# A token mixer beside routed experts: router logits in fp32, another order of VectorE's work, and a last step in halves

## The chip, the core and the metric

The kernel runs on one core of a Trainium2 chip. The metric is the device time of one execution in microseconds (us). The core has TensorE (PE, matrix products), VectorE (DVE), ScalarE (ACT), GpSimd (POOL) and SyncE (SP); each works through its own queue in order, and semaphores tie the queues together.

## The reference, cut to what matters

The input is x of shape (16, 256, 128): 4096 tokens of 128 channels. It is layer-normed to xn. Two branches read xn, and out = x + s * silu(f).

```python
# branch f: four rounds of routed experts, on cur (4096 x 128), starting at xn
for r in range(4):
    logits = cur @ Wg[r] + bg[r]                     # 4 experts
    vals, idx = top_k(logits, 2); w = softmax(vals)  # cw: w at idx, 0 elsewhere
    hmid = gelu(einsum('nh,ehf->enf', cur, W1) + b1) # all 4 experts, 512 wide
    y = einsum('enf,efh->enh', hmid, W2) + b2
    cur = cur + einsum('ne,enh->nh', cw, y)
# branch s, for each of the 16 sequences: r, w, k, v, alpha, g are linear maps of
# xn mixed with its predecessor; state = state * decay + alpha*k*v along time;
# mixed = r * state, normed in groups of 8 channels, times g, then @ W_out.T + b_out
```

Everything is fp32.

## The kernel before

The tokens form 8 blocks of 512 (two sequences each). `cur` holds the state of the experts' branch, channels on partitions, tokens along the row. A **turn** is one round on one block: 32 turns, k = 0 to 31, the eight blocks in order four times. A turn has four **steps**, one for each expert: 128 steps, s = 4k + e. Products are in fp32r, a form of fp32 with fewer bits that TensorE takes at full pace; to keep precision each operand is split into a high and a low part (`cur_hi`, `cur_lo`, `g_hi`, `g_lo`, `w1_hi`, `w1_lo` and so on), and three products of parts are added: hi*hi, lo weights*hi, hi weights*lo.

One step s:
- TensorE `up(s)`: 12 matmuls of 128x512 into the four banks `hb`.
- ScalarE `hidden(s)`: four gelu (L382), two copies to `g_hi` of 1024 columns (L386), in two halves; between the halves it does other small work: `router_tanh`, `end_tanh`.
- VectorE `g_low_half(s, 0)` and `(s, 1)` (L619): `g_lo` = g - `g_hi`.
- TensorE `down(s)` (L909, L910, L914): 12 matmuls into `yb[s % 2]`, the eight with `g_hi` first, then the four with `g_lo`. It waits for `combine(s - 2)`, which frees the bank.
- VectorE `combine(s)` (L633): (y + b2) times the expert's gate, broadcast over partitions in `cw_b`, into `tmp`; a DMA from GpSimd's queue adds `tmp` into `cur` (L322). The last two steps are added by VectorE (L642).

TensorE's queue in step s is `up(s+1)`, then for the late steps `turn_product`, then `down(s)`, then `logits(n)` at the steps of `LOGITS_AT`, then one stage of the mixer. VectorE's queue in step s is the norm statistics of the first steps, `split_cur`, mixer work, `g_low_half(s+1, 0)`, `g_low_half(s+1, 1)`, `router_scores`, `router_gates`, `combine(s)`. The queues are written out by hand; the tables `LOGITS_AT`, `SPLIT_AT`, `NORM_SCALE` say at which step something stands.

**The router.** Turns are taken in batches (`BATCHES`): two of two turns, seven of four. `logits(n)` does, for each turn of a batch, two matmuls of 128x512 with `wg_pad`: the gate weights' high and low parts, 8 columns, stand in 128 columns of zeros, and a shifted window puts turn i's rows at partition 32i of `rb`, all turns adding up in one bank. `router_scores(n)` (L579 to L598) transposes `rb` in blocks of 32x32, adds the two parts and the bias, ranks the experts; `router_tanh` and `router_gates` make the gates; DMAs on SP's queue (`spread_gates`) write them to a scratch and broadcast them into `cw_b`. The logits batches stand at steps 0, 6, 12, 28, 44, 60, 76, 92 and 108; scores are made one step later, gates two steps later. combine(0) and combine(8), the first steps whose gates come from the first two batches, are done at the end of the following step (`LATE`).

**The mixer.** Each sequence m goes through 8 stages, one a step, from step 15 + 7m: three projections into `pb`, the scan (stage 3), the group norm `mixer_norm` (stage 4, some 20 small VectorE instructions), the gate and the output projection (stage 6). Stage 0 of a sequence shares a step with stage 7 of the one before.

**The end of a block.** In the last round, block b is final after step 103 + 4b. `end_tanh(b)` on ScalarE, `end_scaled(b)` and `end_product(b)` on VectorE make z = s * silu(f), `turn_product(b)` on TensorE transposes it into `rb`, `end_output(b)` adds x, and SP's queue stores it. For b = 0 to 6 these stand at steps 101 + 4b (tanh), 102 + 4b (scaled, product) and 103 + 4b (turn, output), among the steps of the next block but one that is still computed. Block 7's follow behind step 127.

## Time and profile before

| | us |
|---|---|
| median of 3 runs | 824.88 |
| lowest and highest | 821.72, 825.96 |
| the profiled execution | 823.14 |
| its span, first to last instruction | 821.3 |
| TensorE busy | 803.9 |
| VectorE busy | 714.8 |
| ScalarE busy | 652.2 |

A profile is one execution. Busy time is the time in which at least one instruction of the engine runs; a matmul's end is modelled, and matmuls overlap, so the pace of TensorE is read from the starts. The mean granted clock of TensorE is 0.993 of full.

### The profile page before, as it was taken

How to read it: one execution, taken by the hardware profiler on the slowest of the kernel's cores; microseconds unless marked ns; L12 is line 12 of the kernel's file. 1: busy time of each engine (PE TensorE's matmuls, PEld its weight loads, DVE VectorE, ACT ScalarE, POOL GpSimd, SP SyncE). 2: the span in 40 equal slices, each digit the busy share in tenths (PEclk: the TensorE clock that was granted, in tenths of full speed). 3: DMA queues.
4: the chain of work that ended last, by engine and by line, in shares of the span. 5: the costliest groups of instructions: out<-in, count | busy, mean ns of one | idle time of the engine just before them, and what ended most of it. 6: DMA issues, size and time to landing. Idle time of an engine off the chain costs nothing. (4 is left out here: it accounts for less than half of the span.)

```text
span 821.3 us, 10635 instructions
## 1 busy us (share of the span) xinstructions
PE 803.9 (98%) x3656; PEld 651.3 (79%) x3656; DVE 714.8 (87%) x1339; ACT 652.2 (79%) x911; POOL 115.0 (14%) x135
## 2 busy tenths in 40 slices
PE   8899999999999999999999999999999999899996
PEld 7787788888788887888888887888878888678885
DVE  6978888889997979988898898898989898889897
ACT  7798887887887877888788886888778887678874
POOL 0010211111111111111111101111111111011110
PEclk9999999999999999999999999999999999999998
DMA  9333463342533415423164422644226343174532
GB/s 255 116 78 91 102 162 84 96 97 39 143 59 83 97 33 142 103 49 94 29 152 100 95 39 39 142 103 104 39 54 164 93 116 72 19 180 115 129 65 51
DMA packets 44468, 78.50 MB, mean 96 GB/s; under 512 B 6656, under 2 KB 23552, under 8 KB 40448
## 3 DMA queue, kind: packets, MB, share of 16 engines
q0 software_dynamic: 18144, 33.04, 23.9%
q1 hardware_dynamic: 25136, 44.64, 16.5%
q8 instruction: 29, 0.48, 0.2%
q10 hardware_dynamic: 1136, 0.16, 0.1%
q14 instruction: 23, 0.19, 0.1%
HBM read 40.34 MB, written 2.36 MB: 52 GB/s over the span
## 5 line engine op out<-in xcount | busy, mean ns | idle before, releaser
L382 ACT ACTIVATE g<-h_bank,b_c 128x512 f32<-128x512 f32 x512 | 329.3, 681 | 80.2 <-PE h_bank L853 78.5
L619 DVE TENSOR_TENSOR g_lo<-g,g_hi 128x1024 fp32r<-128x1024 f32 x256 | 307.9, 1221 | 73.6 <-ACT g_hi L386 72.6
L386 ACT ACTIVATE g_hi<-g 128x1024 fp32r<-128x1024 f32 x256 | 271.7, 1062 | 8.1
L322 POOL DMA_DIRECT2D cur<-tmp x126 | 113.9, 904 | 692.1 <-DVE tmp L633 572.4
L849 PE MATMUL h_bank<-cur_hi,w_hi 128*128 128x512 f32 x512 | 206.3, 403 | 1.2 <-ACT g L382 0.7
L909 PE MATMUL y_bank<-g_hi,w_hi 128*128 128x512 f32 x512 | 203.4, 397 | 2.8 <-issue 2.2
L853 PE MATMUL h_bank<-cur_lo,w_hi 128*128 128x512 f32 x512 | 204.1, 399 | 0.0
L850 PE MATMUL h_bank<-cur_hi,w_lo 128*128 128x512 f32 x512 | 203.1, 397 | 0.0
L910 PE MATMUL y_bank<-g_hi,w_lo 128*128 128x512 f32 x512 | 203.0, 397 | 0.0
L914 PE MATMUL y_bank<-g_lo,w_hi 128*128 128x512 f32 x512 | 140.9, 396 | 2.2 <-DVE g_lo L619 2.2
L909 PEld LDWEIGHTS y_bank<-g_hi,w_hi 128*128 128x128 f32 x512 | 96.5, 188 | 26.5 <-issue 2.6
L914 PEld LDWEIGHTS y_bank<-g_lo,w_hi 128*128 128x128 f32 x512 | 96.3, 188 | 26.2 <-DVE g_lo L619 3.1
L853 PEld LDWEIGHTS h_bank<-cur_lo,w_hi 128*128 128x128 f32 x512 | 96.6, 189 | 23.7 <-DVE cur_lo L567 0.4
L910 PEld LDWEIGHTS y_bank<-g_hi,w_lo 128*128 128x128 f32 x512 | 96.6, 189 | 23.4
L849 PEld LDWEIGHTS h_bank<-cur_hi,w_hi 128*128 128x128 f32 x512 | 97.0, 189 | 20.5 <-ACT g L382 1.1
L850 PEld LDWEIGHTS h_bank<-cur_hi,w_lo 128*128 128x128 f32 x512 | 96.7, 189 | 19.2
L633 DVE SCALAR_TENSOR_TENSOR tmp<-y_bank,b_c,cw_b 128x512 f32<-128x512 f32 x128 | 94.9, 743 | 1.4 <-DMA cur<-tmp 1.3
L653 DVE SCALAR_TENSOR_TENSOR xm<-xx,mix,xn_t 128x256 f32<-128x256 f32 x96 | 42.0, 479 | 0.6
L661 DVE TENSOR_TENSOR xm_lo<-xm,xm_hi 128x512 fp32r<-128x512 f32 x48 | 33.2, 693 | 1.6
L853 PE MATMUL p_bank<-xm_lo,pj_hi 128*128 128x256 f32 x96 | 27.6, 288 | 0.9 <-DVE xm_lo L661 0.9
L849 PE MATMUL p_bank<-xm_hi,pj_hi 128*128 128x256 f32 x96 | 27.5, 286 | 0.8 <-DVE xm_hi L659 0.8
L850 PE MATMUL p_bank<-xm_hi,pj_lo 128*128 128x256 f32 x96 | 27.0, 281 | 0.0
(120 smaller groups left out, 516.9 us busy)
## 6 DMA issues: line engine op xcount, KB each, us to landing
cur<-tmp POOLq DMA_DIRECT2D x126, 256.0 KB, 3.4
cw_b<-cw_scratch SPq DMA_DIRECT2D x31, 1024.0 KB, 5.1
cur<-in_x SPq DMA_DIRECT2D x8, 256.0 KB, 5.5
xn_t<-cur SPq DMA_DIRECT2D x8, 256.0 KB, 2.8
xr<-in_x SPq DMA_DIRECT2D x8, 256.0 KB, 3.2
out<-o SPq DMA_DIRECT2D x7, 256.0 KB, 2.4
cw_b<-in_w SPq DMA_DIRECT2D x4, 256.0 KB, 5.2
cw_b<-cw_scratch SPq DMA_DIRECT2D x1, 768.0 KB, 5.2
```

Source lines behind the costliest of these rows:

```text
L322: pool.dma_start(cur[:, block_of(s // E)], tmp[:, s % 2, :], accum_op=ALU.add).then_inc(summed, DMA)
L382: nc.scalar.activation(g[:, gb, ft * BLK:(ft + 1) * BLK], hb[ft][:, :], ACT.Gelu_apprx_tanh, bias=b1_c[:, e * FT + ft:e * FT + ft + 1]).th ...
L386: nc.scalar.activation(g_hi[:, gb, h], g[:, gb, h], ACT.Copy).then_inc(g_hi_done, 1)
L619: nc.vector.tensor_tensor(g_lo[:, gb, h], g[:, gb, h], as_f32(g_hi[:, gb, h]), ALU.subtract).then_inc(g_lo_done, 1)
L633: nc.vector.scalar_tensor_tensor(out=tmp[:, s % 2, :], in0=yb[s % 2][:, :], scalar=b2_c[:, e:e + 1], in1=cw_b[:, q, e * BLK:(e + 1) * BLK] ...
L653: last = nc.vector.scalar_tensor_tensor(out=xm[:, n, :], in0=xx[:, :], scalar=mix[:, k:k + 1], in1=xs[:, 1:LEN + 1], op0=ALU.mult, op1=ALU ...
L849: nc.tensor.matmul(out_ap, w_hi, v_hi, start=True, stop=False)
L850: nc.tensor.matmul(out_ap, w_lo, v_hi, start=False, stop=False)
L853: return nc.tensor.matmul(out_ap, w_hi, v_lo, start=False, stop=True)
L909: nc.tensor.matmul(yb[b][:, :], w2_hi[:, e * FT + ft, :], hi, start=(ft == 0), stop=False)
L910: nc.tensor.matmul(yb[b][:, :], w2_lo[:, e * FT + ft, :], hi, start=False, stop=False)
L914: last = nc.tensor.matmul(yb[b][:, :], w2_hi[:, e * FT + ft, :], g_lo[:, b, ft * BLK:(ft + 1) * BLK], start=False, stop=(ft == FT - 1))
```

## The change

- `logits(n)`: instead of two fp32r matmuls with 128 columns of weights a turn, one fp32 matmul with 32 columns (`wg_p`: the 4 gate weights and zeros) reads `cur` itself and writes to the partitions 32i to 32i + 31 of `rb`. The split of the gate weights, the copies into `wg_pad` and one add in `router_scores` are gone.
- VectorE's order: combine(0) stands ahead of the norm statistics of step 1, combine(8) between the two `g_low_half` of step 9. low_w2(2) and router_gates(0) stand at the start of step 0. router_scores (for n >= 3) and `end_scaled` stand between the two halves, `end_product` behind them, and both end pieces one step earlier, at 101 + 4b; `turn_product` and `end_output` move to step 102 + 4b. In step 110, the one step with a mixer norm two steps after a logits batch, `mixer_norm` goes behind the `g_low_half`.
- The last step: `down_last` makes the 512 tokens in two halves of 256, the first in `yb[1]`, the second in `hb[3]`, and combine, add, tanh, scale, product, transposes follow by halves; the output was by halves already.

```diff
+def behind_router(s):
+    return s - 2 in LOGITS_AT.values()
...
+        last_y = (yb[(STEPS - 1) % 2], hb[FT - 1])
...
-            if s > END_FROM and (s - END_FROM) % E == 3:
+            if s > END_FROM and (s - END_FROM) % E == 2:
                 r_jobs["end", (s - END_FROM) // E] = len(r_jobs)
...
+            act.wait_ge(r_full, r_jobs["end", NB - 3] + 1)
+            for n in range(2):
+                h = slice(n * HALF, (n + 1) * HALF)
+                act.wait_ge(half_added, n + 1)
+                nc.scalar.activation(th[:, (NB - 1) % 2, h], cur[:, TOK - BLK + n * HALF:TOK - BLK + (n + 1) * HALF], ACT.Tanh,
+                                     scale=0.5).then_inc(half_th, 1)
...
-                if k == 0 or k % NB == QUADS - 1 and k > NB:
-                    nc.vector.tensor_scalar(wg_pad[:, WG_AT:WG_AT + 2 * E], as_f32(wg_hl[:, k // NB, :]), 1.0, None,
-                                            ALU.mult)
...
-                link(nc.vector.tensor_tensor(l3, lgt[p, :, 0:E], lgt[p, :, E:2 * E], ALU.add))
-                link(nc.vector.tensor_tensor(l3, l3, bg3, ALU.add))
+                link(nc.vector.tensor_tensor(l3, lgt[p, :, 0:E], bg3, ALU.add))
...
-                if s >= STEPS - ADDED_BY_DVE:
+                if s == STEPS - 2:
                     last = cur[:, block_of(k)]
                     dve.wait_ge(summed, DMA * (STEPS - ADDED_BY_DVE))
                     dve.wait_ge(combined, s + 3)
-                    if s > STEPS - ADDED_BY_DVE:
-                        dve.wait_ge(added, s - STEPS + ADDED_BY_DVE)
...
+            def combine_half(n):
+                k, e = TURNS - 1, E - 1
+                q = k % 2
+                dve.wait_ge(half_down, n + 1)
+                dve.wait_ge(cwb_ready[q], DMA * (k // 2 + 1))
+                dve.wait_ge(summed, DMA * (STEPS - ADDED_BY_DVE))
+                part = tmp[:, (STEPS - 1) % 2, n * HALF:(n + 1) * HALF]
+                nc.vector.scalar_tensor_tensor(out=part, in0=last_y[n][:, 0:HALF], scalar=b2_c[:, e:e + 1],
+                                               in1=cw_b[:, q, e * BLK + n * HALF:e * BLK + (n + 1) * HALF],
+                                               op0=ALU.add, op1=ALU.mult).then_inc(half_combined, 1)
+                last = cur[:, TOK - BLK + n * HALF:TOK - BLK + (n + 1) * HALF]
+                dve.wait_ge(added, 1)
+                dve.wait_ge(half_combined, n + 1)
+                nc.vector.tensor_tensor(last, last, part, ALU.add).then_inc(half_added, 1)
...
+            def scale_half(n):
+                sx = xn_t[:, SEQS - 2 + n, 1:LEN + 1]
+                dve.wait_ge(p_empty, p_job(SEQS - 1, J_S) + 1)
+                dve.wait_ge(half_added, n + 1)
+                nc.vector.scalar_tensor_tensor(out=sx, in0=cur[:, TOK - BLK + n * HALF:TOK - BLK + (n + 1) * HALF], scalar=0.5,
+                                               in1=sx, op0=ALU.mult, op1=ALU.mult).then_inc(half_scaled, 1)
+            def product_half(n):
+                t2 = th[:, (NB - 1) % 2, n * HALF:(n + 1) * HALF]
+                dve.wait_ge(half_th, n + 1)
+                dve.wait_ge(half_scaled, n + 1)
+                nc.vector.scalar_tensor_tensor(out=t2, in0=t2, scalar=1.0, in1=xn_t[:, SEQS - 2 + n, 1:LEN + 1],
+                                               op0=ALU.add, op1=ALU.mult).then_inc(half_z, 1)
...
-            for off, width in ((0, WG_AT), (WG_AT + 2 * E, 128 - 2 * E)):
-                nc.vector.tensor_scalar(wg_pad[:, off:off + width], ident[:, 0:width], 0.0, None, ALU.mult)
+            nc.vector.tensor_scalar(wg_p[:, :, E:RP], ident[:, 0:R * (RP - E)].rearrange("p (r c) -> p r c", r=R), 0.0, None,
+                                    ALU.mult)
...
-            nc.vector.tensor_scalar(wg_hl[:, :, 0:E], wg_c[:, :, :], 1.0, None, ALU.mult).then_inc(wg_split, 1)
-            dve.wait_ge(wg_split, 1)
-            nc.vector.tensor_tensor(wg_hl[:, :, E:2 * E], wg_c[:, :, :], as_f32(wg_hl[:, :, 0:E]),
-                                    ALU.subtract).then_inc(wg_split, 1)
-            dve.wait_ge(wg_split, 2)
+            nc.vector.tensor_scalar(wg_p[:, :, 0:E], wg_c[:, :, :], 1.0, None, ALU.mult)
...
-                if s == 2:
+                if s == 0:
+                    low_w2(2)
+                    router_gates(0)
+                elif s == 2:
                     norm_root(NORM_GROUPS[1])
...
-                if s > END_FROM and (s - END_FROM) % E == 2:
-                    end_scaled((s - END_FROM) // E)
-                    end_product((s - END_FROM) // E)
...
-                    elif stage == 4:
+                    elif stage == 4 and not behind_router(s):
                         mixer_norm(m)
                     elif stage == 6:
                         mixer_gate(m)
...
                 for half in range(2):
                     if s + 1 < STEPS:
                         g_low_half(s + 1, half)
-                    if half == 0 and s == 0:
-                        router_gates(0)
+                    if half == 0:
+                        if s == 9:
+                            combine(8)
+                        for n in at_step(LOGITS_AT, s - 1):
+                            if n >= 3:
+                                router_scores(n)
+                        if s > END_FROM and (s - END_FROM) % E == 1:
+                            end_scaled((s - END_FROM) // E)
                 if s == 0:
-                    low_w2(2)
                     low_w2(3)
                 elif s == 1:
+                    combine(0)
                     norm_stats(NORM_GROUPS[1])
                     norm_spread(NORM_GROUPS[1])
                 for k in at_step(SPLIT_AT, s):
                     if k < NB // 2:
                         split_cur(k)
-                if s > END_FROM and (s - END_FROM) % E == 3:
+                if s > END_FROM and (s - END_FROM) % E == 1:
+                    end_product((s - END_FROM) // E)
+                if s > END_FROM and (s - END_FROM) % E == 2:
                     end_output((s - END_FROM) // E)
-                for n in at_step(LOGITS_AT, s - 1):
-                    if n >= 3:
-                        router_scores(n)
+                for m, stage in mixers_at(s):
+                    if stage == 4 and behind_router(s):
+                        mixer_norm(m)
                 for n in at_step(LOGITS_AT, s - 2):
                     if n >= 3:
                         router_gates(n)
-                if s - 1 in LATE:
-                    combine(s - 1)
-                if s not in LATE:
+                if s not in LATE and s < STEPS - 1:
                     combine(s)
...
-            end_scaled(NB - 1)
-            end_product(NB - 1)
+            for n in range(2):
+                combine_half(n)
+            for n in range(2):
+                scale_half(n)
+            for n in range(2):
+                product_half(n)
...
+            def down_last():
+                s = STEPS - 1
+                e, b = s % E, s % 2
+                pe.wait_ge(combined, s + 1)
+                pe.wait_ge(gelu_done, FT * (s + 1))
+                for n in range(2):
+                    for ft in range(FT):
+                        if n == 0 and ft % 2 == 0:
+                            pe.wait_ge(g_hi_done, 2 * s + ft // 2 + 1)
+                        hi = g_hi[:, b, ft * BLK + n * HALF:ft * BLK + (n + 1) * HALF]
+                        nc.tensor.matmul(last_y[n][:, 0:HALF], w2_hi[:, e * FT + ft, :], hi, start=(ft == 0), stop=False)
+                        nc.tensor.matmul(last_y[n][:, 0:HALF], w2_lo[:, e * FT + ft, :], hi, start=False, stop=False)
+                for n in range(2):
+                    for ft in range(FT):
+                        if n == 0 and ft % 2 == 0:
+                            pe.wait_ge(g_lo_done, 2 * s + ft // 2 + 1)
+                        lo = g_lo[:, b, ft * BLK + n * HALF:ft * BLK + (n + 1) * HALF]
+                        last = nc.tensor.matmul(last_y[n][:, 0:HALF], w2_hi[:, e * FT + ft, :], lo,
+                                                start=False, stop=(ft == FT - 1))
+                    last.then_inc(half_down, 1)
...
             def logits(n):
                 first, turns = BATCHES[n]
                 pe.wait_ge(r_empty, r_jobs["logits", n])
+                if first < NB:
+                    pe.wait_ge(p_empty, first + turns)
                 for i in range(turns):
-                    pe.wait_ge(cur_split, 2 * (first + i + 1))
-                    w = wg_pad[:, WG_AT - RP * i:WG_AT - RP * i + 128]
-                    q = (first + i) % SPLITS
-                    nc.tensor.matmul(rb[:, :], w, cur_lo[:, q, :], start=(i == 0), stop=False)
-                    last = nc.tensor.matmul(rb[:, :], w, cur_hi[:, q, :], start=False, stop=(i == turns - 1))
+                    pe.wait_ge(cur_split, 2 * (first + i) + 1)
+                    last = nc.tensor.matmul(rb[RP * i:RP * (i + 1), :], wg_p[:, first // NB, :], cur[:, block_of(first + i)],
+                                            start=True, stop=True)
                 last.then_inc(r_full, 1)
...
-                if s > END_FROM and (s - END_FROM) % E == 3:
+                if s > END_FROM and (s - END_FROM) % E == 2:
                     turn_product((s - END_FROM) // E)
-                down(s)
+                if s < STEPS - 1:
+                    down(s)
+                else:
+                    down_last()
...
-            pe.wait_ge(z_ready, NB)
-            for t in range(TPB):
-                ins = nc.tensor.transpose(hb[t // 2][:, t % 2 * D:(t % 2 + 1) * D], th[:, 1, t * D:(t + 1) * D],
-                                          ident[:, :])
-                if t % 2 == 1:
-                    ins.then_inc(half_turned, 1)
+            for n in range(2):
+                pe.wait_ge(half_z, n + 1)
+                for t in range(2):
+                    col = n * HALF + t * D
+                    ins = nc.tensor.transpose(hb[n][:, t * D:(t + 1) * D], th[:, (NB - 1) % 2, col:col + D], ident[:, :])
+                ins.then_inc(half_turned, 1)
```

## Rows read from the trace of the kernel before

**Rows 1.** The page, part 1: busy us, share of the span, instructions
```profile
PE 803.9 (98%) x3656; PEld 651.3 (79%) x3656; DVE 714.8 (87%) x1339; ACT 652.2 (79%) x911; POOL 115.0 (14%) x135
```

**Rows 2.** Groups by form: shapes xcount | busy us, mean ns | idle before
```profile
L927 PE MATMUL r_bank<-cur_hi,wg_pad 128*128 128x512 f32 x32 | 12.6, 395 | 0.0
...
L871 PE MATMUL r_bank<-ident,th 128*128 128x128 f32 x28 | 4.2, 272 | 0.0
```

**Rows 3.** Timeline near step 110: start, us, what, xcount [idle before <-releaser]
```profile
702.40 1.23 DVE L619 TENSOR_TENSOR g_lo<-g,g_hi 128x1024 fp32r<-128x1024 f32 x1 [1.54 <-ACT g_hi L386]
...
703.54 0.71 DVE L579 STREAM_TRANSPOSE lgt<-r_bank 128x512 f32<-128x512 f32 x1
...
704.85 0.39 PE L909 MATMUL y_bank<-g_hi,w_hi 128*128 128x512 f32 x1
...
706.78 0.74 DVE L633 SCALAR_TENSOR_TENSOR tmp<-y_bank,b_c,cw_b 128x512 f32<-128x512 f32 x1
...
707.65 0.39 PE L849 MATMUL h_bank<-cur_hi,w_hi 128*128 128x512 f32 x1
...
710.45 0.60 PE L871 MATMUL r_bank<-ident,th 128*128 128x128 f32 x4
...
713.46 2.35 DVE L619 TENSOR_TENSOR g_lo<-g,g_hi 128x1024 fp32r<-128x1024 f32 x2
...
714.74 0.74 PE L914 MATMUL y_bank<-g_lo,w_hi 128*128 128x512 f32 x2 [1.83 <-DVE g_lo L619]
```

**Rows 4.** TensorE's waits: us in total, times, longest us
```profile
PE y_bank L914 <- DVE g_lo L619: 2.2, 2, 1.8
PE y_bank L909 <- issue: 2.2, 1, 2.2
...
PE p_bank L879 <- DVE st L673: 0.9, 1, 0.9
PE p_bank L853 <- DVE xm_lo L661: 0.9, 4, 0.2
PE p_bank L849 <- DVE xm_hi L659: 0.8, 1, 0.8
...
PE y_bank L909 <- DVE tmp L633: 0.6, 1, 0.6
```

**Rows 5.** Windows: us, each engine busy, PEclk is the granted clock
```profile
34.30:37.70 3.40, 3.40 (x10) 2.63 (x9) 3.06 (x14) 0.14 (x1) 1.01 (x1) 0.50 0.93 304
...
717.00:720.40 3.40, 3.40 (x10) 2.62 (x9) 3.40 (x4) 1.83 (x3) 0.86 (x1) 0.51 0.55 96
```

**Rows 6.** Timeline, 26 to 35 us, and a DMA issue by size and landing
```profile
27.29 0.35 SPq L262 DMA_DIRECT2D cw_b<-cw_scratch  x1
...
30.36 1.63 DVE L504 BATCH_NORM_STATS2 stats<-cur 128x6 f32<-128x128 f32 x8
...
33.08 1.41 DVE L633 SCALAR_TENSOR_TENSOR tmp<-y_bank,b_c,cw_b 128x512 f32<-128x512 f32 x2
...
33.93 0.47 PE L909 MATMUL y_bank<-g_hi,w_hi 128*128 128x512 f32 x1 [2.15 <-issue]
...
cw_b<-cw_scratch SPq DMA_DIRECT2D x1, 256.0 KB, 3.7
```

**Rows 7.** Timeline, around the steps 117 and 126
```profile
756.36 2.35 DVE L619 TENSOR_TENSOR g_lo<-g,g_hi 128x1024 fp32r<-128x1024 f32 x2
...
758.47 0.40 PE L909 MATMUL y_bank<-g_hi,w_hi 128*128 128x512 f32 x1
...
804.88 1.23 DVE L619 TENSOR_TENSOR g_lo<-g,g_hi 128x1024 fp32r<-128x1024 f32 x1 [1.19 <-ACT g_hi L386]
...
807.34 0.39 PE L909 MATMUL y_bank<-g_hi,w_hi 128*128 128x512 f32 x1
```

**Rows 8.** Timeline, the end of the kernel
```profile
814.12 0.74 DVE L633 SCALAR_TENSOR_TENSOR tmp<-y_bank,b_c,cw_b 128x512 f32<-128x512 f32 x1
...
818.92 0.41 ACTq L469 DMA_DIRECT2D out<-o  x1
```

More of the change, by code:

```diff
@@ L26 @@
 QUADS = 4
-WG_AT = (QUADS - 1) * RP
 MIX_FROM, MIX_EVERY = 15, 7
@@ L30 @@
 ADDED_BY_DVE = 2
+HALF = BLK // 2
 P_R, P_W, P_K, P_V, P_A, P_G = range(6)
@@ L93, in mixer_gated_experts @@
         wg_c = sb("wg_c", [128, R, E])
-        wg_hl = sb("wg_hl", [128, R, 2 * E], f32r)
-        wg_pad = sb("wg_pad", [128, WG_AT + 128], f32r)
+        wg_p = sb("wg_p", [128, R, RP])
         b1_c = sb("b1_c", [128, E * FT])
@@ L157, in mixer_gated_experts @@
         made, gates_padded, edge_zeroed = sem("made"), sem("gates_padded"), sem("edge_zeroed")
-        wg_split = sem("wg_split")
         w1_high, w2_high, mixw_high = sem("w1_high"), sem("w2_high"), sem("mixw_high")
@@ L182, in mixer_gated_experts @@
         added = sem("added")
+        half_down, half_combined, half_added = sem("half_down"), sem("half_combined"), sem("half_added")
+        half_th, half_scaled, half_z = sem("half_th"), sem("half_scaled"), sem("half_z")
         half_turned, half_done, last_stored = sem("half_turned"), sem("half_done"), sem("last_stored")
@@ L412, in end_tanh @@
             def end_tanh(b):
-                if b == NB - 1:
-                    act.wait_ge(added, ADDED_BY_DVE)
-                else:
-                    act.wait_ge(summed, DMA * (STEPS - E * (NB - b - 1)))
+                act.wait_ge(summed, DMA * (STEPS - E * (NB - b - 1)))
                 if b >= 2:
@@ L466, in _ @@
                     hidden(s + 1, between)
-            end_tanh(NB - 1)
+            act.wait_ge(r_full, r_jobs["end", NB - 3] + 1)
[4 more added lines that the diff above has]
+                                     scale=0.5).then_inc(half_th, 1)
             act.wait_ge(half_done, 2)
@@ L708, in end_scaled @@
                 dve.wait_ge(p_empty, p_job(2 * b + 1, J_S) + 1)
-                if b == NB - 1:
-                    dve.wait_ge(added, ADDED_BY_DVE)
-                else:
-                    dve.wait_ge(summed, DMA * (STEPS - E * (NB - b - 1)))
+                dve.wait_ge(summed, DMA * (STEPS - E * (NB - b - 1)))
                 nc.vector.scalar_tensor_tensor(out=sx, in0=cur[:, block_of(b)].rearrange("p (b t) -> p b t", b=2),
```

## The prediction

> **What bounds the kernel now.** I read the page first. TensorE is busy for 98% of the span [rows 1], and its clock is granted in full nearly everywhere. So two things alone move the end: the time that TensorE's own instructions take, and the places where it stops. The listing by form gives its instructions for the router's logits [rows 2], the timeline gives their true pace: the twelve 128x512 fp32r matmuls of one down product start between 704.85 and 707.65, where the next group starts, so one costs 0.233 us (its own 0.39 us overlap the next one's) [rows 3]. Then I read TensorE's waits [rows 4]. There are few, all on VectorE or on what VectorE releases: 2.2 + 2.2 + 0.9 + 0.9 + 0.8 = 7.0 us in nine places. Those are times behind a modelled end; each also loses the 0.16 us by which a matmul's 0.39 us are longer than its 0.233, 1.4 us in all, so 8.4 us; with one more of 0.6 us before the down product of step 10 (the row whose releaser is `tmp`) it is 9.2. The windows show what two of them cost further: behind the stop that ends at 33.93 the granted clock is 0.50 for 3.4 us, that is 1.2 GHz and not 2.4 [rows 5], and the same happens once more, from 717.0 to 720.4, behind the stop that ends at 714.74. Half of 3.4 us is lost each time, 3.4 us together. What VectorE's faults cost TensorE is thus 12.6 us. VectorE's and ScalarE's busy time by itself bounds nothing.
>
> **The DVE order, what it gives back.** At the start, TensorE stands 2.15 us before the down product of step 2, because combine(0) runs at 33.08; ahead of it in VectorE's queue stand the statistics that begin at 30.36, and the gates' broadcast that it needs was issued at 27.29 and takes 3.7 us, so it was there at 31.0 [rows 6]. The change puts combine(0) ahead of the statistics: it can run at about 31.0 and end near 31.8, and TensorE's idle time begins at 33.93 - 2.15 = 31.8. Stop and clock loss both go. Late in the kernel the router's scores (703.54 to 706.78, 3.2 us), then combine, end work and mixer norm hold g_lo of step 111 until 713.46, and TensorE waits 1.83 us for it [rows 3]. In the new order the scores run between the two g_lo halves, where VectorE was idle for 1.54 us anyway [rows 3], and the norm goes behind both halves. The waits for `st`, `xm_hi` and `xm_lo` [rows 4] lie in the steps after a router's scores, are 0.2 to 0.9 us long, and their work starts about 1.0 to 1.5 us earlier (the idle time that the scores now fill, and the add of 0.2 us that is gone). combine(8), between the halves of step 9, covers the 0.6. I take all 12.6 us; the least that I can defend is the two long stops with their clock, 2 x (2.2 + 1.7) = 7.8. The moved low_w2(2) and router_gates(0) change places with work of equal length in a stretch where TensorE does not wait. The removed wg_pad copies and the second add (0.2 us for each router) are off TensorE's path and count as nothing; that holds while VectorE is ahead, and they would be worth under 3 us if it never were.
>
> **The DVE order, what it costs.** The turn of the end blocks comes one step earlier: TensorE now needs end_product right behind up(s+1) of step s = 102, 106, ... 126, before down(s). VectorE must have done g_lo's second half and then end_product (0.65 us, the pace of VectorE's 512-column steps: two combines run in 1.41 [rows 6]; a g_lo half paces at 1.15, two in 2.35 [rows 3]). In step 126 g_lo ends at 806.11 and TensorE reached that place at 807.34: 0.6 us of margin [rows 7]; five of the seven steps are like this, with 0.5 to 1.1 us. Two are not. In step 109 the queue behind the first half is scores 3.0, end_scaled 0.65, g_lo 1.15, end_product 0.65: from 702.40 - 1.54 = 700.9, where the first half ends, to 706.35, and TensorE is there at 704.85 [rows 3]: 1.5 us. In step 117 the mixer norm stands ahead of both g_lo halves, which start at 756.36; with end_scaled between and end_product behind they end at 760.0, and TensorE is there at 758.47 [rows 7]: 1.5 us. Behind the turn wait down(s) and everything else in TensorE's queue, so these 3.0 us count in full. end_output also comes a step earlier, behind the g_lo halves, where nothing waits for it.
>
> **The tail.** From the last combine at 814.12 to the last DMA issue at 818.92 [rows 8] all is one chain: combine, add, scale, product, transposes, output, each on 512 columns. By halves the columns are the same and the fixed part is paid twice (0.39 us of a 128x512 matmul stand beside 0.23 of pace; on VectorE a 512-column step paces at about 0.65), but ScalarE, TensorE and VectorE overlap, and the first combine starts when half of the columns are down, 0.5 us earlier. VectorE has eight steps of about 0.4 us on halves where it had four of 0.75: little less. The transposes of half a block replace four in a row. I take 0.8 us of gain; bounds are 0 and 1.3.
>
> **The logits.** Now: 64 matmuls, 32 on the row shown and 32 on its twin for `cur_lo` [rows 2], x 0.233 = 14.9 us, all on TensorE's path. After: 32 matmuls of plain fp32, 32 columns of weights, each turn of a batch into its own 32 partitions; 7 batches of four, 2 of two. No row shows such a matmul. The nearest is the plain fp32 transpose: four run in 0.60 us and one alone takes 0.27 [rows 2, 3], so each paces at 0.11 us for 128 columns, 0.44 us for 512, nearly twice the fp32r pace per column. A true fp32 product also needs both parts of the weights, so two such passes, 0.88 us. From below: one pass and all side by side; from above: four passes at 0.233, 0.93 us each, strictly in a row. In between: if the four go to different parts of the array and only passes of the same turn must follow each other, the second pass of one turn runs beside the first of the next: (n+1) passes for n turns, 7 x 5 x 0.44 + 2 x 3 x 0.44 = 18.0 us. Changing the shape of the work at both ends of nine batches may empty the array: 0 to 0.16 us each (the same difference as above), 0 to 2.9 us, I take 1.5. So 19.5 - 14.9 = +4.6 us. The Trainium skill, "FP8 and Floating Point Precision", TensorE Precision Notes, says that a true fp32 product is four passes through the array; by it a strict queue gives 32 x 4 x 0.233 = 29.8 us. "TensorEngine Tiling (Array Packing)", Key Properties, says that a change of tiling mode drains TensorE, which speaks against this change; no row here shows a tiled matmul.
>
> **The sum.** The profiled execution took 823.1 us, 821.3 of them span. 823.1 - 12.6 + 3.0 - 0.8 + 4.6 = 817.3. The median of the runs is 1.7 above the profiled one; the runs spread over 4 us, so I lean slightly up: 817.5. About 0.5% (4.1 us) is what can be told from no change, so faster means below 820.8 and slower above 829.0.
>
> **Rivals.**
> (a) The quadrants run strictly one after another. Place: the nine logits batches. Price: 32 x 0.9 us plus the full 2.9 for the switches is 31.7 against 14.9, +16.8 us, and the time is 823.1 - 12.6 + 3.0 - 0.8 + 16.8 = 829.5: slower. It decides against the change from 0.89 us a matmul on; at 0.88 with half of the switches it is 827.5. For it: every matmul of this trace follows its predecessor at full length. Against: none of them uses a part of the array.
> (b) A batch runs wholly side by side: 9 x 0.88 + 1.5 = 9.4, -5.5 us, 807.2. This is what the Trainium skill, "TensorE: Matmul & The Clock Gate", Part 3, would have for small tiles: a pack takes one matmul's time plus some nanoseconds a tile. Against: two passes of one turn share a part, and order is kept.
> (c) One pass of 0.44 does the product: 32 x 0.44 + 1.5 = 15.6, +0.7, 813.4. Against: the weights' low part must be used somewhere.
> (d) The earlier turn eats the gain: VectorE is 1 us later in the five steps with margin too, and the two stops of 1.5 us each halve the clock (1.7 us each): 817.3 + 5 x 0.5 + 3.4 = 823.2, no change. For it: margins of 0.5 us, and the clock falls behind stops of about 2 us [rows 4, 5]. Against: the parts of VectorE's work that would delay the five steps were moved away from them, and no stop of 1.5 us stands in this trace to say what the clock does.
> (e) The reorder gives back only the 7.8: 817.3 + 4.8 = 822.1.
>
> **Chances.** Forecast 0.40 (own range 812 to 822); (a) 0.28; (b) 0.12; (c) 0.08; (d) 0.07; (e) 0.05. The range leaves out the far side of (a) and of (b): 806.5 to 829. Faster: 0.37 of the forecast, (b), (c) and a little of (e), 0.59. Slower: the upper half of (a) and some of (d), 0.16. Same: 0.25.
>
> **What would show it.** Logits: a batch of four occupies TensorE for 2.2 us (forecast), 3.6 (a), 0.9 (b). Stops: no wait before the down products of steps 2 and 10, clock 1.00 behind 31 us, no wait for g_lo at step 111; new waits of 1.5 us for `th` in steps 110 and 118 and none in the other five. Tail: last combine to last issue 4 us instead of 4.8. The prediction is wrong above all if the batch's time is another, 7 times its error; then if one of the clock losses stays or the early turn waits in more than two steps.

## The result, and the profile after

The changed kernel takes 809.1 us (median of 4 runs, 808.85 to 809.94), the kernel before 824.8 us (4 runs beside it). The ratio is 0.982, with a 95% interval of 0.981 to 0.984. By the medians it is 15.7 us less, where the forecast had 7.3. The time lies in the stated range. The profiled execution of the changed kernel took 809.94 us, 13.2 less than that of before.

The page of the changed kernel, part 1, the row that answers to [rows 1]:

```profile
PE 794.2 (98%) x3668; PEld 639.0 (79%) x3668; DVE 712.0 (88%) x1328; ACT 652.7 (81%) x912; POOL 114.5 (14%) x135
```

TensorE is still the bound, at the same share; its busy time fell by 9.7 us and the span by 13.2. Both parts have to be explained: less work, and fewer stops.

TensorE's waits in the changed kernel (us in total, times, longest us), beside [rows 4]:

```profile
PE r_bank L909 <- DVE th L737: 4.1, 3, 1.5
...
PE p_bank L901 <- ACT o L365: 2.1, 1, 2.1
```

Not one of the six kinds of stop in [rows 4] is left. In their place stand three waits for `th`, the product of an end block, before a turn. The row between the two is the wait for block 7's product at the very end, 2.6 us. The wait for `o` stands before the transposes of the first block's input, behind the first loads. In this execution `o` starts at 10.38 us, in that of experiment 11 (the same kernel) at 9.79, and the wait is 2.1 us against 0.8. Here a stretch at the lower clock follows, which the execution of 11 lacks:

```profile
12.05:15.46 3.41, 3.24 (x10) 2.35 (x9) 3.31 (x7) 3.35 (x7) 0.00 (x0) 0.50 1.23 290
```

The clock is the third number from the right. Such a stretch costs 1.7 us. Some executions of a kernel have it and some do not, so a difference of about 1 us between two medians of four runs is not firm.

The logits in step 28, timeline of TensorE (start, duration, what, count):

```profile
191.99 0.40 PE L952 MATMUL y_bank<-g_lo,w_hi 128*128 128x512 f32 x1
192.32 0.64 PE L986 MATMUL r_bank<-cur,wg_p 128*32 128x512 f32 x4
```

```profile
192.32 1.06 PE L986 MATMUL r_bank<-cur,wg_p 128*32 128x512 f32 x8
193.31 0.38 PE L887 MATMUL p_bank<-go_hi,wo_hi 128*128 128x256 f32 x1
193.53 0.28 PE L888 MATMUL p_bank<-go_hi,wo_lo 128*128 128x256 f32 x1
```

The first fence shows the records up to 192.6 us, the second those that run at 192.7 or later. Four turns are eight matmul records, since each fp32 matmul shows as two. The first four together take 0.64 us where one of them takes 0.62: they start within 0.02 us of each other. The other four follow, and the next work starts at 193.31, 0.99 us after the first. A batch of two takes as long, 0.98. The trace has 64 such records, two for each of the 32 turns, and the nine batches take 8.9 us from first start to next start, where 64 matmuls of fp32r took 14.9 [rows 2].

That is not yet the whole price. The first record starts 0.33 us behind the last one of the work ahead, where 0.23 is the pace. The second record behind the batch comes 0.22 us after the first, where 0.12 is the pace. From 191.99 to 193.53 it is 1.54 us, and 0.35 without a batch, so a batch occupies TensorE for 1.15 to 1.20 us, in all nine 10.6. A batch of four took 1.86 before and a batch of two 0.93. So a batch of four is about 0.7 us cheaper and a batch of two about 0.25 us dearer, and the logits by themselves give 4.2 us.

The Trainium skill, "TensorE: Matmul & The Clock Gate", Part 3, says that small tiles in different parts of the array run concurrently, a few nanoseconds apart; the trace agrees, with fp32 operands and two passes.

Places of the start and of step 109, in the timeline of VectorE:

```profile
31.61 0.74 DVE L638 SCALAR_TENSOR_TENSOR tmp<-y_bank,b_c,cw_b 128x512 f32<-128x512 f32 x1
32.27 1.64 DVE L513 BATCH_NORM_STATS2 stats<-cur 128x6 f32<-128x128 f32 x8
...
688.53 0.71 DVE L585 STREAM_TRANSPOSE lgt<-r_bank 128x512 f32<-128x512 f32 x1
...
691.51 0.68 DVE L729 SCALAR_TENSOR_TENSOR xn_t<-cur,xn_t 128x512 f32<-128x512 f32 x1
692.11 1.22 DVE L624 TENSOR_TENSOR g_lo<-g,g_hi 128x1024 fp32r<-128x1024 f32 x1
693.24 0.68 DVE L737 SCALAR_TENSOR_TENSOR th<-th,xn_t 128x512 f32<-128x512 f32 x1
```

combine(0) is at 31.61, ahead of the statistics, and TensorE does not stop (compare [rows 6]). The windows show its clock from 30 to 38 us, 1.00:

```profile
30.00:38.00 8.00, 8.00 (x36) 6.45 (x35) 7.22 (x31) 6.09 (x9) 1.01 (x1) 1.00 0.75 224
```

The clock loss of [rows 5] is gone, here and behind step 111. The last rows of VectorE show step 109 in the order that the forecast wrote down: scores from 688.53 to 691.5, end_scaled, g_lo, end_product, ready at 693.9.

### The profile page after: what moved, and what is told of

It reads as the page before. It is cut to its first block, busy times and chain, and to the rows that moved or that the text cites. A ratio compares the mean times of both kernels' runs of the same rounds, so it can differ in the third digit from the quotient of the medians.

```text
span 808.1 us, 10652 instructions
## 1 busy us (share of the span) xinstructions
PE 794.2 (98%) x3668; PEld 639.0 (79%) x3668; DVE 712.0 (88%) x1328; ACT 652.7 (81%) x912; POOL 114.5 (14%) x135
## 4 chain that ended last, share of the span: by engine, by line
PE 91%; DVE 3%; DMA 3%; ACT 1%; issue 1%; SPq 0%; DVEq 0%; ACTq 0%; POOLq 0%
PE h_bank L887 14%; PE h_bank L891 14%; PE y_bank L952 14%; PE y_bank L948 14%; PE y_bank L947 14%; PE h_bank L888 14%; DMA cur<-tmp 2%; PE p_bank L887 2%; PE p_bank L891 2%; PE p_bank L888 2%; PE r_bank L986 1%; PE p_bank L917 1%; DMA cw_b<-in_w 1%; DVE g_lo L624 1%; ACT g L389 1%
## 5 line engine op out<-in xcount | busy, mean ns | idle before, releaser
L947 PE MATMUL y_bank<-g_hi,w_hi 128*128 128x512 f32 x508 | 201.1, 396 | 0.0
L948 PE MATMUL y_bank<-g_hi,w_lo 128*128 128x512 f32 x508 | 200.6, 395 | 0.0
```

The source lines that it names most:

```text
L947: nc.tensor.matmul(yb[b][:, :], w2_hi[:, e * FT + ft, :], hi, start=(ft == 0), stop=False)
L948: nc.tensor.matmul(yb[b][:, :], w2_lo[:, e * FT + ft, :], hi, start=False, stop=False)
```

## The experiments

All ratios are to the kernel before, timed on the same chip beside the runs. The medians of the kernel before were 823.4 us beside the first four, 824.8 beside the next four, 824.4 beside the last three. Where a time is compared with the changed kernel, the 809.1 us were measured at another time than the runs of experiments 1 to 8, so such a difference can be off by about as much as these medians differ, 1.4 us.

### 1. The fp32 logits alone

```diff
 # the kernel before, with:
-                    nc.tensor.matmul(rb[:, :], w, cur_lo[:, q, :], start=(i == 0), stop=False)
-                    last = nc.tensor.matmul(rb[:, :], w, cur_hi[:, q, :], start=False, stop=(i == turns - 1))
+                    last = nc.tensor.matmul(rb[RP * i:RP * (i + 1), :], wg_p[:, first // NB, :], cur[:, block_of(first + i)],
+                                            start=True, stop=True)
...
-                link(nc.vector.tensor_tensor(l3, lgt[p, :, 0:E], lgt[p, :, E:2 * E], ALU.add))
-                link(nc.vector.tensor_tensor(l3, l3, bg3, ALU.add))
+                link(nc.vector.tensor_tensor(l3, lgt[p, :, 0:E], bg3, ALU.add))
```

> The kernel before with the fp32 logits alone (one fp32 matmul of 32 weight columns a turn into its own 32 partitions; the split of the gate weights, the copies and the second add gone), everything else as before. Theory 1 (the turns of a batch run side by side, two passes of about 0.45 us in all): TensorE spends 9 x 0.98 = 8.8 us on logits instead of 64 x 0.233 = 14.9, so up to 6.1 us less, 818.7; the stops for VectorE behind a router remain and may eat 1 to 2 us of it, since TensorE comes 0.9 us sooner: 818.5 to 821. Theory 2 (the changed logits are worth nothing by themselves, the gain of the change is the order): 823 to 825.

817.4 us (816.9 to 819.4), ratio 0.993 (0.991 to 0.995): 6.0 us less. Theory 1 holds and theory 2 falls; the time is 1.1 us below the range given for theory 1. The stops of the kernel before are all there still:

```profile
PE y_bank L905 <- DVE g_lo L614: 2.0, 2, 1.6
PE y_bank L900 <- issue: 1.8, 1, 1.8
...
PE p_bank L840 <- DVE xm_hi L654: 0.7, 2, 0.6
PE p_bank L870 <- DVE st L668: 0.7, 1, 0.7
```

They did not grow although TensorE comes sooner. With 0.3 for `tmp` they add up to 6.4 us, 7.6 before [rows 4], so 1.2 of the 6.0 us are shorter stops and 4.2 are the batches themselves. That the add and the copies taken from VectorE are what shortened them was not tried.

### 2. The same fp32 matmuls in the full array

```diff
-                    last = nc.tensor.matmul(rb[RP * i:RP * (i + 1), :], wg_p[:, first // NB, :], cur[:, block_of(first + i)],
-                                            start=True, stop=True)
+                    last = nc.tensor.matmul(rb[:, :], wg_p[:, WG_AT - RP * i:WG_AT - RP * i + 128],
+                                            cur[:, block_of(first + i)], start=(i == 0), stop=(i == turns - 1))
```

The round's gate weights are copied into the window as the kernel before did, but in fp32 and without a split.

> The changed kernel, with the fp32 logits in the full array: 128 columns of weights, all but 4 of them zeros, in a shifted window, the turns of a batch adding up in the whole bank. Same products, same number of matmuls. Theory 1 (parts of the array run side by side): now nothing can, each fp32 matmul takes its two passes of 0.43 to 0.45 us alone, 3.5 us a batch of four and 1.7 us a batch of two instead of 0.98, 7 x 2.5 + 2 x 0.75 = 19 us more, 828. Rival (fp32 matmuls are cheap in any shape, and the parts don't matter): no change, 809.

824.8 us (823.6 to 826.7), ratio 1.001 (1.000 to 1.003): 15.7 us more than the changed kernel, all that the whole change gained. The logits of step 28, timeline of TensorE:

```profile
195.54 3.59 PE L987 MATMUL r_bank<-cur,wg_p 128*128 128x512 f32 x8
198.57 0.68 PE L888 MATMUL p_bank<-go_hi,wo_hi 128*128 128x256 f32 x1
199.09 0.28 PE L889 MATMUL p_bank<-go_hi,wo_lo 128*128 128x256 f32 x1
```

Eight passes one after the other, (3.59 - 0.59) / 7 = 0.43 us each. So the pass of 0.43 us, which the forecast took from the fp32 transposes as 0.44, is right, and the gain comes from the parts of the array. The price is 15.7 and not 19. The record at 198.57 starts early, but it is 0.68 us long and the one behind it comes 0.52 us later instead of 0.12: the next work waits for the last pass here too. Read to the second record behind the batch, as above, a batch of four takes 3.43 us here and 1.19 in the changed kernel, a batch of two 1.71 and 1.19. Over nine batches that is 16.8 us. The expectation was too high because it priced a batch in parts at its passes alone, 0.98 us, and left out the 0.2 us at its two ends.

### 3. The new order and the halves with the logits of before

```diff
 # the changed kernel, with the kernel before's logits(n), wg_hl, wg_pad, their copies and both adds
```

> The changed kernel with the logits of before (fp32r, two matmuls a turn, wg_pad, both adds), so the new order and the halves alone. Theory 1: 6.1 us more than the changed kernel, 815, and against the kernel before 9 to 10 us less, since the stops behind the routers and the clock losses are gone. Theory 2 (the order carries all): 809 to 811.

814.3 us (813.7 to 815.3), ratio 0.989 (0.986 to 0.991): 9.1 us less than before, 5.2 more than the changed kernel. The starts of `up` in the steps 30 and 94, first this kernel, then the changed one:

```profile
194.55 0.40 PE L897 MATMUL h_bank<-cur_hi,w_hi 128*128 128x512 f32 x1
...
588.67 0.40 PE L897 MATMUL h_bank<-cur_hi,w_hi 128*128 128x512 f32 x1
```

```profile
193.77 0.39 PE L887 MATMUL h_bank<-cur_hi,w_hi 128*128 128x512 f32 x1
...
584.83 0.40 PE L887 MATMUL h_bank<-cur_hi,w_hi 128*128 128x512 f32 x1
```

The distance grows from 0.78 to 3.84 us over the four batches between, 3.1 us. The batches themselves, read as above, differ by 0.66 us (steps 44 and 92) and 0.71 (steps 60 and 76), 2.7 of the 3.1. Over all nine they give 4.2 of the 5.2 us; where the other 1.0 lies was not found. A batch in parts takes its 0.99 us of passes, some 0.1 us ahead of them and some 0.1 behind them. The Trainium skill, "TensorEngine Tiling (Array Packing)", Key Properties, says that a change of tiling mode drains TensorE; the trace agrees in kind, the drain is these 0.2 us for two changes.

### 4. The turn behind the down product

```diff
+                down(s)          # down_last() in the last step
                 if s > END_FROM and (s - END_FROM) % E == 2:
                     turn_product((s - END_FROM) // E)
-                down(s)
```

> The changed kernel, with turn_product behind down(s) and not ahead of it in steps 102 to 126. In the changed kernel TensorE starts the turns of steps 110, 114 and 118 1.4, 1.7 and 1.5 us late, waiting for the product. If those stops are lost time, it is 4.5 us less, 804.6, and TensorE waits for th nowhere but at the end. Rival (VectorE or the accumulating DMAs are the limit there, and the stop only moves to g_lo or to the down product): 808 to 809.

806.6 us (806.2 to 807.6), ratio 0.979 (0.978 to 0.981): 2.5 us less than the changed kernel, not 4.5. The waits for `th` in the middle are gone; some of TensorE's waits that remain are new:

```profile
PE p_bank L917 <- DVE mn L708: 0.6, 1, 0.6
PE p_bank L887 <- DVE xm_hi L678: 0.5, 1, 0.5
```

There is one of 0.2 us for `xm_lo` as well. With 0.16 us more for each behind a modelled end, 1.8 us come back as waits for mixer work in the steps 111 and 114. So most of the stop was lost time, and some of it moved. With that of 5, which cannot be told from it, this is the fastest kernel of the study.

### 5. end_output last in VectorE's step, on top of 4

```diff
-                if s > END_FROM and (s - END_FROM) % E == 2:
-                    end_output((s - END_FROM) // E)
...
                 if s not in LATE and s < STEPS - 1:
                     combine(s)
+                if s > END_FROM and (s - END_FROM) % E == 2:
+                    end_output((s - END_FROM) // E)
```

> The kernel with the turn behind down(s), and also end_output at the very end of VectorE's step (behind norm, gates and combine). With the turn behind down(s), end_output waits for it and holds up what stands behind it in VectorE's queue: TensorE stopped 0.6 us for mn at step 111 and 0.5 + 0.2 us for xm_hi and xm_lo at step 114. If end_output is what holds them, these stops go: 806.6 - 1.0 = 805.6. Rival (VectorE is simply full there): 806.5.

806.9 us (805.9 to 807.4), ratio 0.978 (0.977 to 0.980): no difference from kernel 4 that can be told. The profile is finer: the wait for `mn` is gone, as expected, the wait of 0.5 us for `xm_hi` at step 114 stays, and the start of `up` in the last steps is about 0.5 us earlier. Half of the expectation fell: at step 114 it is not end_output that holds VectorE.

### 6. combine(0) behind the statistics again

```diff
                 elif s == 1:
-                    combine(0)
                     norm_stats(NORM_GROUPS[1])
                     norm_spread(NORM_GROUPS[1])
...
+                if s == 1:
+                    combine(0)
```

> The changed kernel with combine(0) behind the norm statistics of step 1, where it was before. The forecast priced the early combine(0) at 2.3 us of stop and 1.7 us of clock: 809.1 + 4.0 = 813.1, a stop of about 2 us before the down product of step 2 and a granted clock of 0.5 for 3.4 us behind it. Rival (the clock loss would come anyway, or the stop is made good by later slack): 810 to 811.

813.7 us (812.3 to 814.1), ratio 0.986 (0.985 to 0.987): 4.6 us more than the changed kernel by the medians. The one run with a mean clock of 0.998 took 812.25 us, 3.3 more than the 808.9 of the changed kernel's runs at 0.999, so the price is 3.3 to 4.6 us. The stop is back (timeline of TensorE), and so is the low clock behind it (a window's row):

```profile
35.49 0.47 PE L948 MATMUL y_bank<-g_hi,w_hi 128*128 128x512 f32 x1 [1.83 <-issue]
```

```profile
36.59:40.00 3.41, 3.41 (x10) 2.63 (x9) 3.17 (x10) 0.00 (x0) 0.40 (x1) 0.50 0.73 197
```

### 7. Each logits matmul twice in a row

```diff
+                    for _ in range(2):
-                    last = nc.tensor.matmul(...)
+                        last = nc.tensor.matmul(...)   # same operands, same result
```

> The changed kernel with each turn's logits matmul issued twice in a row with the same result (turn 0, turn 0, turn 1, turn 1, ...). If each 32-partition part of the array has its own order and the parts do not wait for one another, a batch of four takes four passes of about 0.44, 1.9 us, and so does a batch of two: 9 x 0.9 = 8 us more, 817. If the queue's order binds (a turn cannot start before the last matmul of the turn ahead has started, as the forecast assumed), the second matmul of a turn runs beside the first of the next and a batch of four takes about 5 x 0.87 = 4.4 us: 7 x 3.4 + 2 x 1.6 = 27 us more, 836.

816.7 us (2 runs, 816.2 and 817.1), ratio 0.990 (0.988 to 0.992): 7.6 us more than the changed kernel, as the first theory had it (817) and not the second (836). Step 28:

```profile
194.41 1.94 PE L987 MATMUL r_bank<-cur,wg_p 128*32 128x512 f32 x16
196.29 0.38 PE L887 MATMUL p_bank<-go_hi,wo_hi 128*128 128x256 f32 x1
```

Sixteen passes in 1.9 us, four at a time. In the program turn 0's second matmul stands ahead of turn 1's first, and turn 1 does not wait for it: the four turns' first passes start within 0.04 us of each other, and the next four start 0.45 us later. Each part of the array keeps its own order, and the queue's order between parts does not make one wait for another. By the forecast's assumption the batch would have taken 4.4 us.

### 8. The router's scores behind both halves again

```diff
-                        for n in at_step(LOGITS_AT, s - 1):   # between the halves
-                            if n >= 3:
-                                router_scores(n)
...
+                for n in at_step(LOGITS_AT, s - 1):           # behind both, and behind end_output
+                    if n >= 3:
+                        router_scores(n)
```

> The changed kernel with router_scores (n >= 3) behind both halves of g_lo again, all else as changed. If the scores between the halves are what removed the stops behind the routers, these come back, 0.6 to 1.3 us each in the four steps 30, 46, 78 and 94, 3 to 4 us in all; at step 110 the stop for the turn becomes shorter by the 3 us of scores, so 1.4 us are won back there: 811. Rival (the other pieces of the new order give enough slack by themselves): 808 to 809.

814.2 us (813.9 to 816.1), ratio 0.987 (0.986 to 0.989): 5.1 us more than the changed kernel, where 2 were expected. TensorE's waits:

```profile
PE p_bank L917 <- DVE mn L708: 2.2, 1, 2.2
PE r_bank L909 <- DVE th L737: 2.1, 2, 1.3
...
PE p_bank L917 <- DVE st L692: 0.7, 1, 0.7
```

The stops behind the routers return almost as in [rows 4], and the turn of step 110 is free, as expected. What was not expected is the first row: with the scores late and the norm behind both halves, `mn` is 2.2 us late for step 111, and the clock behind it is 0.50 from 707.11 to 710.52 us, which takes 1.7 us more. Placing the norm behind the halves is good only with the scores between them; the norm alone in its old place was not tried.

### 9 and 10. The gates of turn 29 ahead of a store and a load

```diff
             for b in range(NB - 1):
+                if b == 2:
+                    spread_gates(END_TURN + 2 + b)
                 store(b)
                 if b + 2 < NB:
                     load_x_again(b + 2)
-                if END_TURN + 2 + b < TURNS:
+                if b != 2 and END_TURN + 2 + b < TURNS:
                     spread_gates(END_TURN + 2 + b)
```

> The changed kernel with one change on SP's queue: the gates of turn 29 are sent ahead of the store of block 2 and the second load of x for block 4. In the changed kernel these two, issued at 704.4 and 704.9, run beside the 1 MB broadcast of the gates of turn 28 (704.04) and the accumulating DMA of step 110 (703.55), which takes 7.5 us to land instead of 3.7; the next accumulation, the tanh of block 3 and the turn at step 114 wait, 1.7 us. If the crowd of transfers is the cause, the accumulation lands in 4 to 6 us and the stop at step 114 shrinks to under 0.5: 1.2 to 1.7 us less, 807.6. Rival (the broadcast alone delays it): the stop stays, 809.

> The same change of SP's queue on the kernel with the turn behind down(s). There the late landing costs TensorE 0.5 + 0.2 us for xm_hi and xm_lo at step 114. Crowd theory: these go, 806.6 - 0.7 = 805.9. Rival: 806.6.

On the changed kernel: 816.4 us (814.9 to 817.1), ratio 0.991 (0.989 to 0.993). On kernel 4: 810.7 us (810.1 to 813.1), ratio 0.985 (0.982 to 0.987). Both are worse, by 7.4 and 4.1 us. In the first of them, timelines of GpSimd's, SP's and ScalarE's queues:

```profile
702.09 0.86 POOL L331 DMA_DIRECT2D cur<-tmp  x1 [7.79 <-DVE tmp L640]
709.73 0.86 POOL L331 DMA_DIRECT2D cur<-tmp  x1 [6.78 <-DMA cur<-tmp]
718.00 0.86 POOL L331 DMA_DIRECT2D cur<-tmp  x1 [7.42 <-DMA cur<-tmp]
```

```profile
702.58 0.33 SPq L270 DMA_DIRECT2D cw_b<-cw_scratch  x1
...
709.38 0.33 SPq L270 DMA_DIRECT2D cw_b<-cw_scratch  x1
```

```profile
717.50 0.63 ACT L426 ACTIVATE th<-cur 128x512 f32<-128x512 f32 x1 [6.47 <-DMA cur<-tmp]
```

Beside the accumulation of 702.09 there were only the broadcast of 702.58 and a write of 8 KB, and the next one still had to wait until 709.73. So the crowd of transfers is not what slows it. The second broadcast, now at 709.38, the store and the load all fall on the next accumulation, which is late as well; the tanh waits 6.5 us and holds up the gelu behind it in ScalarE's queue. In the profile of 9 TensorE stops 3.2 us for that gelu, and then its clock is at the lower level for 10 us, which costs 5.1 us more:

```profile
718.16:728.40 10.24, 9.04 (x23) 6.79 (x24) 7.38 (x11) 7.09 (x10) 1.57 (x2) 0.50 0.30 52
```

In that of 10 the stop is 4.4 us, with 3.4 us at 0.50 behind it. As a cure the move failed.

A broadcast beside an accumulation is not enough either. In the changed kernel (POOL's and SP's queues):

```profile
502.33 1.04 POOL L329 DMA_DIRECT2D cur<-tmp  x1 [5.01 <-DVE tmp L638]
...
502.81 0.32 SPq L270 DMA_DIRECT2D cw_b<-cw_scratch  x1
...
512.17 0.86 POOL L329 DMA_DIRECT2D cur<-tmp  x1 [8.79 <-DMA cur<-tmp]
...
731.78 0.86 POOL L329 DMA_DIRECT2D cur<-tmp  x1 [4.27 <-DVE tmp L638]
...
732.96 0.33 SPq L270 DMA_DIRECT2D cw_b<-cw_scratch  x1
```

The accumulation of 502.33 is issued 0.48 us ahead of the broadcast and takes 9.3 us to land, that of 731.78 is issued 1.18 us ahead of one and takes 3.5. So it is throughout this trace: the eight whose broadcast is issued between 0.34 us before and 0.78 us behind them take 6.7 to 9.3 us, the 22 whose broadcast comes 0.95 to 2.6 us behind them 3.4 to 4.7. What decides seems to be how close the two issues stand; no run moved one of them alone.

### 11. The changed kernel again, beside 9 and 10

> The changed kernel itself, beside the two others on the same chip: 809.1, with stops of 1.4, 1.7 and 1.5 us for th. If the chip differs by more than 1 us from the first time, the differences of the others are read against this one.

809.0 us (808.3 to 810.8), ratio 0.982 (0.980 to 0.984), the same waits for `th` (3.9 us in three). So 9 and 10 can be read against 809.0. This run says nothing of the chips on which 1 to 8 ran.

## Why the prediction was right and where it failed

**What bounds the kernel** was read rightly: TensorE's own time and its stops.

**The logits** are the step that failed, in the sentence "if the four go to different parts of the array and only passes of the same turn must follow each other, the second pass of one turn runs beside the first of the next: (n+1) passes for n turns". It assumed that the queue's order holds across parts. It does not (7): a batch is two passes long, however many turns it has. The rest of the term was right: a pass measured 0.43 for 0.44 (2), two passes a product, and 0.2 us a batch for the change of shape, 1.7 in all for 1.5. In place of 19.5 us the nine batches take 10.6, so in place of +4.6 us stands -4.2. The runs differ by 5.2 (3) and 6.0 (1), the latter with 1.2 us of shorter stops; the forecast's rival (b) had -5.5. The rival was given 0.12, with "order is kept" against it, a reason for which no row stood. That one term is off by 8.8 us and the forecast by 8.4; the other terms are off by 1.5 us and less.

**The order's gains**, forecast at 12.6. The price of the early combine(0) was 4.0 and measured 3.3 to 4.6 (6). Scores between the halves measured 5.1 (8), though the kernel without that move is not simply the old one. All stops of [rows 4] are gone in the changed kernel. As a sum: order and halves measured 9.1 (3); with 1.0 of it from the halves and 4.5 us of new stops against it, that puts the gain at about 12.6. Right, by the sum; the single small stops were not tried one by one.

**The order's costs**, forecast at 3.0 in two stops of 1.5, measured 4.5 in three. The starts on either side of the three are 1.63, 1.92 and 1.72 us apart instead of 0.24, so the three stops cost 1.4, 1.7 and 1.5. Those of steps 110 and 118 came as worked out. That they "count in full" held only in part: with the turn out of the way 2.5 of the 4.5 us came back (4). The third, at step 114, the forecast had waved away among the five with margin. What is late there, in the changed kernel:

```profile
703.55 0.86 POOL L329 DMA_DIRECT2D cur<-tmp  x1 [7.81 <-DVE tmp L638]
704.04 0.33 SPq L270 DMA_DIRECT2D cw_b<-cw_scratch  x1
...
711.53 0.86 POOL L329 DMA_DIRECT2D cur<-tmp  x1 [7.12 <-DMA cur<-tmp]
...
715.11 0.64 ACT L424 ACTIVATE th<-cur 128x512 f32<-128x512 f32 x1 [2.65 <-DMA cur<-tmp]
```

The accumulation of 703.55 is issued 0.49 us ahead of the 1 MB broadcast of the gates and takes 7.5 us to land, where the median of all 126 is 3.4 (the 3.7 in the expectation of 9 is the median of seven around it); the next one starts late, tanh waits for it, and the product and the turn wait for tanh. The kernel before has the same late landing; there the turn stood a step later and it cost nothing. Rival (d) asked about VectorE's lateness and not about that of a DMA. That the clock would fall behind stops of 1.5 us did not come true here: none of the three is followed by a low clock.

**The tail**, forecast at 0.8. Before, the last combine started at 814.12 and the last output was issued at 818.92 [rows 8]. Now:

```profile
800.91 0.64 PE L974 MATMUL h_bank<-g_lo,w_hi 128*128 128x256 f32 x4
801.11 0.48 DVE L655 SCALAR_TENSOR_TENSOR tmp<-y_bank,b_c,cw_b 128x256 f32<-128x256 f32 x1
...
805.73 0.41 ACTq L478 DMA_DIRECT2D out<-o  x1
```

From the first half's combine it is 4.6 us, and that combine starts when the second half's matmuls are still running. Counted from the start of the last matmul (801.28 and 813.50 in the two traces) it is 4.45 instead of 5.42 us, a gain of about 1.0. No run had the halves alone.

**The sum.** With what the traces show in place of three terms it is 823.1 - 12.6 + 4.5 - 1.0 - 4.2 = 809.8, and 809.1 was measured. As runs: the logits alone gave 6.0 (1) and order and halves alone 9.1 (3), together 15.1 us; the changed kernel, which has both, gains 14.3 to 15.7 us, depending on beside which runs of the kernel before one reads.

**Open**: where the other 1.0 us lies that the logits are worth in (3); why an accumulation issued close to a broadcast lands so late; and whether another distance between the two frees step 114.

## What to carry to other kernels

When small outputs of a full contraction go to different groups of 32 partitions, count the passes of one and not of all, and add the change of shape, here 0.2 us a batch: the parts neither wait for each other nor for the queue's order. A turn's fp32 product costs 0.86 us of passes where the two fp32r matmuls cost 0.47. Four turns side by side made fp32 the cheaper form, two did not. Before a consumer is moved a step earlier, list for each instance what it waits for, transfers included, and ask which of them was late already and hidden; and try the consumer behind the next long block of work, not ahead of it, which here gave 2.5 us more.

## What the runs showed of the hardware

- Matmuls of 128x32 weights to four different groups of 32 partitions start 0.01 us apart and run together; an fp32 matmul of 512 columns is two records of 0.43 us pace each. Two turns take as long as four, 0.98 to 1.00 us, and some 0.1 us is lost at either end of such a batch among matmuls of the full array.
- Issued as turn 0 twice, turn 1 twice and so on, the first passes of all four turns still start together (7).
- A 256 KB accumulating DMA lands in 3.4 us (median of 126). Issued between 0.8 us ahead of a 1 MB broadcast from DRAM to all partitions and 0.3 us behind it, it lands in 6.7 to 9.3 us, issued 0.95 to 2.6 us ahead of one in 3.4 to 4.7 (the changed kernel's trace, 8 and 22 of them).
- The length of a stop alone does not tell whether TensorE's granted clock falls behind it. It stayed at 1.00 behind single stops of 1.2 to 1.5 us in the changed kernel and behind one of 1.7 us in 7. It fell behind those of 1.8 us (in 1, in 6 and in the kernel before), of 2.2 us (in 8 and in the kernel before) and also behind one of 1.6 us in 1, which a second one of 0.4 us followed within 1.1 us. Each time it was at 0.50 for 3.4 us, but for 10.2 us behind the stop of 3.2 us in 9. For 1 and for 7, the matmul behind the stop and the row of a window behind it:

```profile
709.14 0.50 PE L905 MATMUL y_bank<-g_lo,w_hi 128*128 128x512 f32 x1 [1.58 <-DVE g_lo L614]
...
711.17:714.58 3.41, 3.41 (x10) 2.63 (x9) 3.41 (x5) 1.47 (x3) 0.86 (x1) 0.50 0.50 72
```

```profile
727.35 0.33 PE L909 MATMUL r_bank<-ident,th 128*128 128x128 f32 x1 [1.71 <-DVE th L737]
...
727.35:734.00 6.65, 6.65 (x34) 5.59 (x35) 6.58 (x11) 5.27 (x8) 1.10 (x2) 1.00 0.27 50
```
